# Sum of values in a graph layer: who multiplies the value rows by their weights, and in how many instructions the one-hots are made

## The reference

```python
score = jnp.einsum('ehc,ehc->eh', q[dst], k[src]) / sqrt(OUT_C)
m = segment_max(score, dst);  p = jnp.exp(score - m[dst])
denom = segment_sum(p, dst);  alpha = p / denom[dst]
msg = v[src] * alpha[:, :, None]
out = jax.ops.segment_sum(msg, dst, num_segments=n)
```

## Time and profile before

| | us |
|---|---|
| median of three runs | 7153.08 |
| lowest, highest | 7152.85, 7164.23 |
| the profiled execution | 7145.89 |
| its span in the profile | 7144.2 |
| the sum of values in it (2724 to 3289) | 565 |

### The profile page before, as it was taken

One profiled execution on the slowest core, in us unless ns is written; L12 is line 12 of the kernel. 1 busy time (PEld: TensorE's weight loads), 2 busy tenths in 40 slices (PEclk: granted clock), 3 DMA queues, 4 the chain that ended last, 5 costly groups with the idle time before them and its releaser, 6 DMA issues. The chain is left out here.

```text
span 7144.2 us, 114758 instructions
## 1 busy us (share of the span) xinstructions
PE 5082.2 (71%) x23608; PEld 3897.9 (55%) x23609; DVE 4037.3 (57%) x10176; ACT 2624.3 (37%) x5843; POOL 3151.9 (44%) x4006
## 2 busy tenths in 40 slices
PE   5666666556666645664467777769999998999986
PEld 3445454234444535553211111159989988889876
DVE  4666666343333347877577777744444455445443
ACT  1111111111111110001078888845555554445433
POOL 3777776027777730000099999921111111112111
PEclk8999988765555556665655555579999999999998
DMA  4333333025555522331112222233333343224331
GB/s 126 98 98 98 98 98 89 15 87 156 158 158 157 157 80 78 97 96 43 29 64 73 73 73 73 74 133 127 142 131 136 128 153 130 109 100 149 123 109 60
DMA packets 523425, 745.71 MB, mean 104 GB/s; under 512 B 57861, under 2 KB 419336, under 8 KB 523240
## 3 DMA queue, kind: packets, MB, share of 16 engines
q1 hardware_dynamic: 440008, 512.24, 21.2%
q0 software_dynamic: 83232, 231.06, 11.4%
HBM read 584.89 MB, written 158.20 MB: 104 GB/s over the span
## 5 line engine op out<-in xcount | busy, mean ns | idle before, releaser
L1956 PE MATMUL ps<-moving,parts 128*128 128x384 f32 (+1 forms) x11662 | 2075.0, 335 | 223.2 <-DVE moving L2162 112.4
L1956 PEld LDWEIGHTS ps<-moving,parts 128*128 128x128 f32 x11662 | 1971.9, 190 | 295.7 <-DVE moving L2162 164.2
L444 POOL DMA_INDIRECT arena<-table_kv,arena x1664 | 1646.8, 990 | 520.4 <-issue 442.9
L2019 ACT ACTIVATE moving<-counts 128x1152 fp32r<-128x1152 uint8 (+1 forms) x952 | 1060.5, 1125 | 684.6 <-PE ps L1956 675.0
L1894 POOL CAST moving<-counts 128x1152 fp32r<-128x1152 uint8 (+1 forms) x357 | 402.9, 1129 | 2034.1 <-PE ps L1956 1985.1
L2162 DVE CAST moving<-counts 128x1152 fp32r<-128x1152 uint8 (+1 forms) x714 | 812.0, 1143 | 562.6 <-PE ps L1956 554.1
L1621 PE MATMUL ps<-arena 128*128 128x392 bf16 x1568 | 769.0, 505 | 372.4 <-POOL arena L1571 278.0
L1571 POOL TENSOR_SCALAR arena<-arena 128x128 bf16<-128x128 f16 x1568 | 1018.7, 663 | 0.1
L1643 ACT ACTIVATE arena<-ps 128x392 uint8<-128x392 f32 x1568 | 824.4, 529 | 334.1 <-PE ps L1621 326.6
L1621 PEld LDWEIGHTS ps<-arena 128*128 128x128 bf16 x1568 | 163.4, 104 | 978.3 <-ACT arena L1643 774.7
L1586 DVE TENSOR_SCALAR arena<-arena 128x392 bf16<-128x392 f16 x1572 | 559.6, 356 | 192.0 <-PE ps L1621 189.9
(11 more groups left out here) (290 smaller groups left out, 5331.9 us busy)
## 6 DMA issues: line engine op xcount, KB each, us to landing
counts<-adjacency SPq DMA_DIRECT2D x105, 2352.0 KB, 8.4
adjacency<-arena SPq DMA_DIRECT2D x784, 98.0 KB, 1.7
edge_values<-arena SPq DMA_DIRECT2D x208, 256.0 KB, 3.2
arena<-edge_values SPq DMA_DIRECT2D x208, 256.0 KB, 3.1
arena<-table_kv,arena POOLq DMA_INDIRECT x1664
counts<-adjacency SPq DMA_DIRECT2D x14, 1568.0 KB, 6.6
table_kv<-arena POOLq DMA_DIRECT2D x14, 896.0 KB, 4.7
rest<-table_norm SPq DMA_DIRECT2D x60, 192.0 KB, 5.3
```

The source lines that it names most:

```text
L444: pool.indirect_dma_start(m.ring4[:, r * HALF + k, 0:f], None, table, bass.IndirectOffsetOnAxis(m.idx4[:, r * HALF + k:r * HALF + k + 1], ...
L1956: mm = pe.matmul(m.bank(g % 2, n * P), d.parts[SOURCE[u]][:, s + q, t_, :], moving[:, q * n * P:(q + 1) * n * P], start=(s + q == 0 and t_ ...
L2019: act.activation(to, of, ACT.Copy).then_inc(by_act, 1)
```

## The change

GpSimd gets a program for the stage. For each half it waits until the products of half j-2 are made (the messages' buffer is free then) and the value rows have landed, and multiplies all four steps' value rows in one instruction of 128x512 elements. VectorE loses both of its multiplications and makes the one-hots of a half in one compare of 128x512 elements by `hits`, behind the first add.

```diff
+        @block.gpsimd
+        def _(pool):
+            def weigh(i, j, r):
+
+                h = r % 2
+                wait(pool, used, (j - 1) * HALF)
+                pool.wait_ge(read[r], 16 * i + 16)
+                pool.tensor_tensor(
+                    m.msg[:, h, :, 0:D].rearrange("p k (n c) -> p k n c", c=C1),
+                    m.ring4[:, r * HALF:(r + 1) * HALF, 0:D].rearrange("p k (n c) -> p k n c", c=C1),
+                    copies(m.weight[:, ds(j * HALF * H1, HALF * H1)].rearrange("p (k n) -> p k n", n=H1), 3, C1),
+                    ALU.mult).then_inc(weighted, 1)
+
+            for r in range(4):
+                weigh(0, r, r)
+            with pool.Fori(1, TURNS // 2) as i:
+                for r in range(4):
+                    weigh(i, 4 * i + r, r)
...
-                    part = slice(k % 2 * 2, k % 2 * 2 + 2)
-                    first_step = j * HALF + k % 2 * 2
-                    if k < 2:
-
-                        op = dve.tensor_tensor(m.hit[:, h, part], copies(m.number[:, :], 1, 2),
-                                               copies(m.local[:, ds(first_step, 2)], 2, P), ALU.is_equal)
-                        if k == 1:
-                            op.then_inc(hit_ready, 1)
-                    else:
-                        if k == 2:
-                            dve.wait_ge(read[r], 16 * i + 16)
-                        op = dve.tensor_tensor(
-                            m.msg[:, h, part, 0:D].rearrange("p k (n c) -> p k n c", c=C1),
-                            m.ring4[:, r * HALF + part.start:r * HALF + part.stop, 0:D].rearrange("p k (n c) -> p k n c", c=C1),
-                            copies(m.weight[:, ds(first_step * H1, 2 * H1)].rearrange("p (k n) -> p k n", n=H1), 3, C1), ALU.mult)
-                        if k == 3:
-                            op.then_inc(weighted, 1)
+                    if k == 0:
+                        hits(dve, m, h, j * HALF).then_inc(hit_ready, 1)
```

## The result

| | before | changed |
|---|---|---|
| median of five runs, us | 7153.08 | 7194.42 |
| lowest, highest | 7150.35, 7164.23 | 7187.14, 7198.25 |
| profiled execution, its span | 7145.89, 7144.2 | 7198.25, 7196.6 |
| the stage, see below | 574.0 | 613.7 |

The ratio is 1.0052, with a 95% interval of 1.0037 to 1.0067: slower, by 41 us between the medians, where 43 were forecast. The two profiled spans differ by 52 us, of which 12 had come up before the stage began; those 12 are a difference between executions, not of the change.

What follows compares the result with a forecast made beforehand. A round of 10.93 us was laid to VectorE's halves, the block-number load and one TensorE wait. Held compares made it 11.75: 52 x 0.82 = 43 us on 7153, forecast 7196 us, range 7145 to 7270.

Steps and rivals of the forecast that it cites:

- The wait that sets a round: TensorE's products of the first half delay the third half's first add, costing 0.55 us once a round before the change.
- C1: First add of the third of a round's four halves (A to D; digits count adds); forecast 4.93 us into the round.
- The pauses: On VectorE, bare adds each wait for the one before: 0.15 us idle, 0.435 us from add to add.
- The table load: Block-number load behind a round's last half: next round's first add 2.10 us behind the fourth add, last half 3.78 us.
- GpSimd's multiplication: One 512-column two-input instruction a half on GpSimd, taken as 1.24 us, between 1.06 and 1.42.
- The collision: VectorE's compare, reading two SBUF inputs, stands until GpSimd's earlier-started multiplication ends, mainly in the third half; round plus 0.82 us.
- TensorE's clock: Products forecast at granted clock 0.50; rival: it rises, removing the 0.55 us wait beside an unheld compare; 0.11 with pause-free adds.
- The sum: Whole stage: 52 rounds at 0.82 us more each, 43 us, giving 7196 us.
- The unheld compare: Rival: the compare starts first and GpSimd stands instead, within its slack; round 10.86 us, time 7149, chance 0.2.
- GpSimd was not slow: Rival: GpSimd's multiplication takes 2.0 us (time 7269) or 2.65 us (7337); chance 0.15.
- The adds did need their pauses: Rival denied here: an add behind an add costs only 0.20 us, time 7101; 0.11 together with the higher TensorE clock.

Runs made afterwards that it cites:

- one compare only: Against the kernel before: one 512-column compare a half behind the first add, VectorE keeps its multiplications, GpSimd idle; stage 603.1 us, 29.1 longer.
- The ramp in PSUM: Changed kernel, its compare reading the node numbers from a copy in PSUM instead of SBUF; stage 574.7 and 574.5 us, against 574.0 before the change.
- the wait for the compare: Changed kernel, with GpSimd's multiplication also waiting for the compare of its half; stage 576.3 us, 2.3 longer than before the change, ratio 1.0022.
- GpSimd in two instructions: Changed kernel, with GpSimd's multiplication split into two instructions of 256 columns each; stage 592.9 us, 18.9 longer than before the change.

## Why the prediction was right, point by point

*The wait that sets a round.* Right. The kernel behaved as one repeated round of four halves. C1 was forecast at 4.93 and came at 4.92, held back by TensorE's products of A; the table load stood in D, where it was read.

*The pauses.* Right, within 0.01 us: A2 at 0.81, A3 0.43 later, B1 at 2.11. The kernel with one compare only shows them alone: 29 us, where I had expected 27 in that run.

*The table load.* Wrong by 0.15 us a round. I had D at 3.78 ahead of the load, it is 3.93. I took the load to start as far behind D4 as it had started behind the last multiplication, 0.25 us; it started 0.42 behind D4, and in the kernel before it had been 0.46 behind D4, with the multiplication in between. So the time from D4 to the next A1 hardly depends on that multiplication: 2.26 us for 2.30. It is 8 us of the sum, and the sum without it came out right only because other terms were too large.

*GpSimd's multiplication.* Mis-sized: 1.24 taken, 1.048 measured. The two ends of the fixed part were 0.19 and 0.55, and I took the middle. With the 617 and 1048 ns of 256 and 512 columns the pace is 431 / 256 = 1.68 ns a column, twice the 0.846 of the cast, with 0.19 fixed. The reading of two inputs at the cast's pace, 1.06, was the right one; its fixed part held too. The 0.19 us less are 10 us of the sum.

*The collision.* Right in direction and mechanism, and in place for a round with TensorE at the lower clock. GpSimd started 0.04 us ahead of the add and not at the same moment, the compare 0.24 behind it, and the following add 0.46 behind GpSimd's end, as read from the other stage's pair. The adds, which have one of their two inputs in PSUM, were not held: 254 began inside a multiplication of GpSimd, and none took over 0.30 us. The ramp in PSUM shows the cause, the wait for the compare shows that without the overlap nothing is lost, and GpSimd in two instructions shows how long it lasts. Missed was that TensorE's clock moves the collision. The forecast has all products at 2.12 us and D's compare held by 0.03. In 18 rounds they were faster and D's was held by 0.5 to 0.7. A's compare was held 4 times, by GpSimd's multiplication for B, where the forecast had GpSimd finish first. The held time was 31 us in C, 12 in D and 3 in A; 74 compares of 208 and at most 1.38 us, where one in four and 1.6 were forecast. The time hit the forecast all the same because a hold in D takes the place of a wait ahead of C.

*The sum.* 0.82 us a round forecast, 0.76 measured (11.68 less 10.92), 39.7 for 43 us in all. Several errors nearly cancelled (estimates in us, each from its size in the round and how often it came): the table load (+8), GpSimd's length (-10), its start 0.04 us ahead of C1 (-2), D's hold in the typical round (-2) and the four held compares of A (+3). That the median hit within 2 us of 7196 is luck in that part.

*The rivals.* The unheld compare did not come: there were 0.24 us between the two starts, more than the 0.20 reckoned. GpSimd was not slow. The adds did need their pauses. TensorE's clock did come up in some rounds, but not so as to shorten the round: its mean over the stage was 0.61 after the change, 0.64 before.

## What to carry to other kernels

When work moves from VectorE to GpSimd, look at what VectorE runs at that moment: here a `tensor_tensor` with both inputs in SBUF stood until the GpSimd instruction that had started ahead of it was over (1.34 us for 0.68), and two engines released by the same semaphore met in every round. Put one input in PSUM, or let the two miss each other where there is slack. And count what an instruction hides before merging or moving it: behind a dependent chain, here adds that wait for each other, an instruction that fills the pause costs only the difference, and taking it away may give nothing or less.

## What the runs showed of the hardware that I had not expected

- A two-input 32-bit multiplication on GpSimd took 1.68 ns a column and 0.19 us fixed (617 ns for 256, 1048 for 512), twice the 0.846 ns a column of its one-input cast, within 1%.
- GpSimd's second instruction did not slip in ahead of a compare that had been waiting: the two took turns (compare 0.92, GpSimd up to 1.16 us).
- Reading one input of the compare from PSUM cost nothing: 684 ns from either place.
- How long a held compare took depended only on where it began: it ended 0.55 us behind GpSimd's end whether it had begun 0.25 or 0.50 us into the multiplication, and one that began 0.9 us into it took its usual 0.68.
